# A graph network's first layer: the edge loop in steps of two groups, with eight gathers in a row

## The chip, the cores and the metric

The kernel runs on one core of a Trainium2 chip. The metric is the device time of one execution in microseconds, the median of several runs. A core has five engines with their own instruction streams: PE (matrix products), DVE (vector), ACT (scalar), POOL (GpSimd) and SP (here it only starts transfers). They meet at semaphores: an instruction adds one (`then_inc`) when it is done, and another engine's instruction waits until a count is reached (`wait_ge`). An indirect DMA, the gather of 128 rows by a list of indices, is issued by POOL, which generates its descriptors.

## The reference

Two graph layers, each followed by a residual sum and a layer norm, over 6250 nodes with 128 values and 100000 edges sorted by their destination. Only the first is touched by the change:

```python
h = x @ W1 + b1
h_i, h_j = h[dst], h[src]
e = concatenate([h_i, h_j - h_i], axis=-1)
m = relu(relu(e @ W2 + b2) @ W3 + b3)
out = relu(segment_max(m, dst, num_segments=N_NODES))
x = layernorm(x + out)
# second layer: segment_sum(edge_weight * x[src]) over dst, times W, plus b
```

## The kernel before

The first product is split: for an edge, `e @ W2` is a sum of p (from the destination) and q (from the source). Both tables are computed once and stored, as `p_tab` and `q_tab`. The 100000 edges are 784 tiles of 128, and four tiles are a group: 196 groups of 512 edges (`G`). The first layer's loop works through them, software-pipelined across the engines. For each group:

- POOL gathers q of the sources, four gathers of 128 rows (L423), into one of 12 ring places (`qg`, `RING`).
- SP loads four windows of p of 128 rows each (64 KB, L494, for the group four ahead), and a row of destinations and segment starts spread over the partitions (128 KB, L479).
- DVE makes a one-hot matrix from that row (`oh`, L888). PE adds the two parts in PSUM (`m_ps`): eight passes of the gathered q through the identity and of the window through the one-hot matrix (L1372, L1373). Its last matmul adds one to `m1_done`.
- ACT applies the relu (L635); PE multiplies by W3 (`z_ps`, L1385); ACT applies the second relu (L640); DVE runs the segmented maximum along the edges (the scan, L989); PE transposes (`t_ps`, L1394); ACT copies (L646) and stores (L650).

Beside it, the same loop prepares the second layer: it sorts edges by the block of their source. DVE makes one-hot matrices of the source block (`blk_oh`, L894). PE counts and ranks with them in `s_ps` (L1346 to L1353). DVE turns the counts into the first row of each block (L900, L905, L910). PE adds these first rows with one more matmul, L1359, `first_b` against three times the identity. DVE picks each edge's place by a product and a sum (L916, L918). Once in four groups five small steps (L941 to L960) split places into rows and columns, in each group L967 makes a one-hot matrix of the rows, and PE moves the edge values to their places (`values`, L1332); DVE sums them up (L973).

Each engine runs its own `step0(i, r)` with its parts at fixed lags, so the order of the instructions is written out by hand. On PE a step is: `gathered` (group r-2), `firsts_added` (r-2), `values` (r-7), `slots` (r-1), `second` (r-3), `by_edge` (r-4). Six of PE's parts end in a release for each group. DVE's `one_hot` waits for `m1_done` of two groups before; POOL waits for `m1_done` of twelve groups before:

```python
for g in range(G):
    if g >= RING:
        pool.wait_ge(m1_done, g - RING + 1)
    for j in range(GT):
        ... indirect_dma_start(...)
```

POOL starts the first 48 gathers once q is stored and the first transposes are copied (`tr_copied`). At that time the preparation is still running: DVE counts and places the destinations (L834 to L860), PE sums over partitions (L1282 to L1286) and moves p's rows to their nodes (L1295), and ACT copies them (L618, L627; the last step adds to `p_ev`, 13 in all). SP then writes `p_tab`, and the loop's windows are read from it.

## Time and profile before

| what | value |
|---|---|
| median of 3 runs | 2623.38 us (2616.09 to 2624.47) |
| profiled execution, its own time | 2633.35 us |
| its span, first to last instruction | 2631.6 us |
| mean granted clock of TensorE | 0.917 of full speed |
| busy: PE, DVE, ACT, POOL | 1940.8, 1619.5, 817.0, 1279.1 us |
| chain that ended last, by engine | PE 43%, issue 19%, SP's queue 11%, another core or unknown queue 9%, DVE 8% |
| gathers L423 | 784, mean 971 ns, idle before them 503.2 us |
| relu L635 | 196, mean 687 ns, idle before them 644.2 us |

A "busy" time adds what an engine ran; the chain follows the last instruction back through what released it. "Remote" is a wait whose end the profile can't tie to an instruction that had just ended; "issue" is idle time in which no wait shows. Of the span, the preparation is roughly the first 215 us, the first layer's loop follows until about 1415 us, and the second layer takes the rest.

### The profile page before, as it was taken

Reading aid. Unit: us, or ns where it says so; the run is one execution under the profiler, and the core shown is the slowest. Engines: PE = TensorE matmul, PEld = TensorE weight load, DVE = VectorE, ACT = ScalarE, POOL = GpSimd, SP = SyncE. Lnnn points to the kernel's source line nnn. Section 1 sums busy time; section 2 is a strip of 40 time slices with the busy share of each in tenths; the row PEclk is TensorE's granted clock in tenths of the full one; section 3 lists DMA queues with packets and bytes.
Section 4 is the critical chain, followed back from the end, with each engine's and each line's share of the span. In section 5 each row is a group of like instructions: output and inputs, shape, how many; then the busy total and the mean of one; then the engine's idle time right before and its main releaser. Section 6 shows DMA issues by size and latency. Waiting matters only on the chain.

```text
span 2631.6 us, 62039 instructions
## 1 busy us (share of the span) xinstructions
PE 1940.8 (74%) x15568; PEld 1701.2 (65%) x15568; DVE 1619.5 (62%) x4450; ACT 817.0 (31%) x2385; POOL 1279.1 (49%) x1300
## 2 busy tenths in 40 slices
PE   4616677777777777777785378888888888788884
PEld 4615565565565555565564378877888778788884
DVE  3416666666666666666679544444444444688887
ACT  0312233233332332332332234445554555100003
POOL 6444566666666666666643435555555555100000
PEclk7757999999999999999997589999999999899997
DMA  4215555555555555555553156766666677788885
GB/s 114 81 46 153 142 148 147 151 148 148 150 147 150 146 150 151 146 148 150 148 147 91 32 179 209 216 207 208 216 214 210 214 214 217 225 268 267 262 266 175
DMA packets 534341, 447.34 MB, mean 170 GB/s; under 512 B 64731, under 2 KB 499383, under 8 KB 534240
## 3 DMA queue, kind: packets, MB, share of 16 engines
q1 hardware_dynamic: 342788, 208.10, 29.1%
q0 software_dynamic: 53312, 138.17, 16.5%
q10 hardware_dynamic: 138140, 100.06, 12.7%
q14 instruction: 78, 0.64, 0.1%
q8 instruction: 23, 0.38, 0.1%
HBM read 300.43 MB, written 145.64 MB: 170 GB/s over the span
## 4 chain that ended last, share of the span: by engine, by line
PE 43%; issue 19%; SPq 11%; another core or an unknown queue 9%; DVE 8%; ACT 3%; DMA 2%; DVEq 2%; POOL 2%; ACTq 1%; POOLq 0%
SPq L494 8%; PE z_ps L1385 5%; PE t_ps L1394 4%; PE m_ps L1372 4%; PE z_ps L1460 4%; PE t_ps L1460 4%; PE m_ps L1484 4%; PE m_ps L1373 4%; PE z_ps L1484 3%; PE t_ps L1484 2%; DVE run L989 2%; POOL whole L430 2%; SPq L490 1%; SPq L483 1%
## 5 line engine op out<-in xcount | busy, mean ns | idle before, releaser
L423 POOL DMA_INDIRECT whole<-q_tab,src_ti x784 | 760.9, 971 | 503.2 <-remote 243.0
L440 POOL DMA_INDIRECT tab<-whole,row_at x392 | 410.1, 1046 | 355.9 <-ACT whole L698 175.3
L1119 DVE TENSOR_SCALAR whole<-row_bc,node_id 128x768 f32<-128x768 uint8 x392 | 233.5, 638 | 390.1 <-PE t_ps L1460 110.4
L1460 PE MATMUL z_ps<-win,whole 128*128 128x128 f32 x2352 | 302.9, 286 | 71.6 <-DVE whole L1119 21.8
L1372 PE MATMUL m_ps<-ident,whole 128*128 128x128 f32 x1568 | 324.3, 290 | 29.1 <-issue 17.1
L635 ACT ACTIVATE m<-m_ps,bias 128x512 f32<-128x512 f32 x196 | 134.7, 687 | 644.2 <-remote 591.9
L1460 PEld LDWEIGHTS z_ps<-win,whole 128*128 128x128 f32 x2352 | 282.7, 198 | 78.0 <-issue 41.6
L1460 PE MATMUL t_ps<-win,whole 128*128 128x128 f32 x2352 | 294.7, 280 | 50.6 <-issue 25.8
L1373 PE MATMUL m_ps<-oh,win 128*128 128x128 f32 x1568 | 316.2, 285 | 0.6 <-issue 0.6
L1460 PEld LDWEIGHTS t_ps<-win,whole 128*128 128x128 f32 x2352 | 274.4, 193 | 54.1 <-issue 30.3
L1372 PEld LDWEIGHTS m_ps<-ident,whole 128*128 128x128 f32 x1568 | 259.1, 207 | 62.6 <-issue 62.5
L1170 DVE TENSOR_TENSOR whole<-whole 128x384 f32<-128x384 f32 x440 | 242.9, 552 | 55.9 <-issue 39.3
L916 DVE TENSOR_TENSOR scratch<-s_ps,blk_oh 128x196 f32<-128x196 f32 x196 | 70.6, 360 | 308.1 <-remote 287.3
L1373 PEld LDWEIGHTS m_ps<-oh,win 128*128 128x128 f32 x1568 | 252.3, 202 | 1.3 <-issue 1.3
L989 DVE TENSOR_TENSOR_SCAN run<-row_bc,run,z_ps 128x512 f32<-128x512 uint8 x195 | 248.4, 1274 | 0.7 <-ACT z_ps L640 0.7
L698 ACT ACTIVATE whole<-z_ps,slot_vals 128x128 f32<-128x128 f32 x588 | 169.5, 378 | 221.5 <-PE t_ps L1460 89.2
L1385 PE MATMUL z_ps<-m,w 128*128 128x512 f32 x392 | 232.6, 677 | 0.0
L1394 PEld LDWEIGHTS t_ps<-ident,run 128*128 128x128 f32 x784 | 111.3, 153 | 187.0 <-issue 169.9
L698 ACT ACTIVATE whole<-t_ps,slot_vals 128x128 f32<-128x128 f32 x588 | 168.5, 388 | 137.4 <-PE t_ps L1460 52.3
L1394 PE MATMUL t_ps<-ident,run 128*128 128x128 f32 x784 | 157.3, 297 | 72.7 <-issue 65.0
L1332 PE MATMUL s_ps<-whole 128*128 128x18 bf16 x784 | 48.5, 171 | 198.1 <-issue 163.7
L1332 PEld LDWEIGHTS s_ps<-whole 128*128 128x128 bf16 x784 | 36.8, 96 | 226.4 <-issue 225.5
(277 smaller groups left out, 3128.3 us busy)
## 6 DMA issues: line engine op xcount, KB each, us to landing
win<-p_tab SPq DMA_DIRECT2D x784, 64.0 KB
seg_tab<-run_e ACTq DMA_DIRECT2D x196, 256.0 KB
win<-xw_tab SPq DMA_DIRECT2D x784, 64.0 KB
whole<-tab SPq DMA_DIRECT2D x220, 200.0 KB
whole<-tab ACTq DMA_DIRECT2D x220, 200.0 KB
row_bc<-seg_row_tab SPq DMA_DIRECT2D x196, 128.0 KB
row_bc<-rel_tab SPq DMA_DIRECT2D x196, 96.0 KB
whole<-q_tab,src_ti POOLq DMA_INDIRECT x784
```

What stands on the lines that cost most here:

```text
L423: pool.indirect_dma_start(qg[:, g % RING, j, :], None, q_tab[:, :], IOA(ap=src_ti[:, t:t + 1], axis=0)).then_inc(q_ld[g % RING], 16)
L440: pool.indirect_dma_start(tab[:, :], IOA(ap=row_at[0:FR, k:k + 1], axis=0), fat[0:FR, k % RR, :], None).then_inc(fat_st[k % RR], 16)
L698: last = nc.scalar.activation(fat[0:FR, GK * (r % UN) + c, q * KW:q * KW + D], fat_bank[r % 2][0:FR, c, q * P:(q + 1) * P], ACT.Copy, scal ...
L989: V.tensor_tensor_scan(run[:, s, :], row_bc[:, r % RB, GE:2 * GE], z_ps[:, s, :], first, ALU.mult, ALU.max).then_inc(run_done, 1)
L1119: last = V.tensor_scalar(pick[:, s, j, :], row_bc[:, r, 0:GK * SLOTS], node_id[:, j:j + 1], None, ALU.is_equal)
L1170: V.tensor_tensor(node_hot[:, r % PS, :, :], node_row[:, ds(at, P)].unsqueeze(1).to_broadcast([P, SL, P]), loaded[:, r % PL, 0:SL * KW].re ...
L1372: mm(m1_ps[:, s, c], lhsT=qg[:, r % RING, j, :], rhs=ident[:], start=True, stop=False)
L1373: last = mm(m1_ps[:, s, c], lhsT=win[:, r % UN, j, :], rhs=oh[:, s, c], start=False, stop=True)
L1385: mm(z_ps[:, s, :], lhsT=w3[:], rhs=m1[:, s, :], start=True, stop=True).then_inc(z_done, 1)
L1394: last = nc.tensor.transpose(t_ps[:, s, c], run[:, s, c], ident[:])
L1460: last = mm(fat_bank[s][0:FR, c, q * P:(q + 1) * P], lhsT=pick[:, s, j, (c * SL + q) * FR:(c * SL + q + 1) * FR], rhs=win[:, r % UN, CK * ...
L1484: last = mm(sum_bank[r % PS], lhsT=node_hot[:, r % PS, q, :], rhs=loaded[:, r % PL, q * KW:q * KW + D], start=q == 0, stop=q == SL - 1)
```

## The change

The loop goes in steps of two groups, a pair. The parts and their arithmetic stay, but these move:

- POOL gathers eight times in a row, and asks for one release a pair: `m1_done` of four pairs before. (A line near the top sets `AHEAD` to 3 and a later line sets it to 4; the loop is built with 4.) It begins when all of `p_ev` has arrived, at the end of p's placement.
- Destination rows are loaded for two groups at once (256 KB) into a ring of six pairs, one-hot matrices are made for two groups at once, the slot work of DVE (counts, first rows, product, sum, small steps, the one-hot matrix of rows) is done for two groups at once, and the small steps come once for a pair.
- The first rows are added on DVE, two additions that read PSUM, and the matmul L1359 with its release is gone.
- On PE a step is `gathered` a and b, `second` of the pair before, `by_edge` and `values` of two before, and `slots` of this pair. `slots` and `values` release once for a pair. DVE's step begins with a wait for the `slots` of the pair before.
- SP writes `p_tab` before it loads the destination rows.

```diff
@@ POOL
-            pool.wait_ge(tr_copied, 1)
...
-            for g in range(G):
-                if g >= RING:
-                    pool.wait_ge(m1_done, g - RING + 1)
-                for j in range(GT):
+            pool.wait_ge(p_ev, HX // GT)
...
+            for u in range(G // 2):
+                if u >= AHEAD:
+                    pool.wait_ge(m1_done, 2 * (u - AHEAD) + 2)
+                for g in (2 * u, 2 * u + 1):
+                    for j in range(GT):
...
@@ SP
-            for g in range(G + LATE):
-                if g + UN < G:
-                    sp.wait_ge(m1_done, g + 1)
-                    windows(p_tab, g + UN)
...
+            for v in range(G // 2 + 2):
+                if 2 * v + UN < G:
+                    sp.wait_ge(m1_done, 2 * v + 2)
+                    for g in (2 * v + UN, 2 * v + UN + 1):
+                        windows(p_tab, g)
+                if v >= 2 and 2 * (v - 2) + RB < G:
+                    sp.wait_ge(run_done, 2 * (v - 2) + 2)
+                    rows0(v - 2 + RB // 2)
@@ ACT
+            def step0(i, w):
+                for h in range(2):
+                    for part, lag in ((relu_1, 1), (relu_2, 2)):
+                        if runs(i, 2 * (w - lag)):
+                            part(i, 2 * (w - lag) + h)
+                if runs(i, 2 * (w - 1)):
+                    many_copy(i, w - 1)
+                for h in range(2):
+                    if runs(i, 2 * (w - 3)):
+                        run_copy(i, 2 * (w - 3) + h)
+                        store(i, 2 * (w - 3) + h)
@@ DVE, first rows and places of a pair
+            def slots_of(i, w):
...
+                V.tensor_tensor_scan(first[...], keep[...], rows3[...], 0.0, ALU.mult, ALU.add).then_inc(slot_step, 1)
+                for s in range(2):
+                    last = V.tensor_tensor(picked[...], s_ps[:, s, 0:GT * NBK]..., first[...], ALU.add)
...
+                V.tensor_tensor(picked[:, :, :], picked[:, :, :], blk_oh[:, a:a + 2, :, :]..., ALU.mult).then_inc(slot_step, 1)
+                V.tensor_reduce(slot_t[...], picked[:, :, :], axis=AX_X, op=ALU.add).then_inc(slot_done, 1)
@@ DVE
+            def step0(i, w):
+                if runs(i, 2 * (w - 1), RING):
+                    dve.wait_ge(slot_ps, pair(i, w - 1) + 1)
+                if runs(i, 2 * (w - 3), RING):
+                    values_sum(i, w - 3)
+                if runs(i, 2 * (w - 1), RING):
+                    slots_of(i, w - 1)
+                if runs(i, 2 * (w - 2), RING):
+                    for h in range(2):
+                        scan(i, 2 * (w - 2) + h)
+                if runs(i, 2 * (w + 1), RING):
+                    one_hot(i, w + 1)
+                    block_hot(i, w + 1)
+                if runs(i, 2 * (w - 1), RING):
+                    slots_placed(i, w - 1)
@@ PE
-            def firsts_added(i, r):
...
-                for part, lag in ((gathered, 2), (firsts_added, 2), (values, PERM_LAG + 1), (slots, 1), (second, 3), (by_edge, 4)):
-                    if runs(i, r - lag, RING):
-                        part(i, r - lag)
+                for part, lag in ((gathered, 0), (second, 1), (by_edge, 2)):
+                    if runs(i, 2 * (w - lag), RING):
+                        for h in range(2):
+                            part(i, 2 * (w - lag) + h)
+                if runs(i, 2 * (w - 2), RING):
+                    values(i, w - 2)
+                if runs(i, 2 * w, RING):
+                    slots(i, w)
```

POOL's stream from its last preparation gathers on, before; L412 is the preparation's gather, L423 the loop's:

```order
L412 DMA slot_vals<-dst_tab,tile_i 128x128 x6
L423 DMA whole<-q_tab,src_ti 128x128 [waits tr_copied,q_st]
L423 DMA whole<-q_tab,src_ti 128x128 x47
L423 DMA whole<-q_tab,src_ti 128x128 [waits m1_done]
L423 DMA whole<-q_tab,src_ti 128x128 x3
```

POOL's stream at the same place after; L419 is the loop's gather:

```order
L408 DMA slot_vals<-dst_tab,tile_i 128x128 x6
L419 DMA whole<-q_tab,src_ti 128x128 [waits p_ev,q_st]
L419 DMA whole<-q_tab,src_ti 128x128 x31
L419 DMA whole<-q_tab,src_ti 128x128 [waits m1_done]
L419 DMA whole<-q_tab,src_ti 128x128 x7
```

The first run goes from 48 gathers to 32 and waits for `p_ev`; each later run goes from four to eight.

PE's stream for one group in the middle of the loop, before, from the end of `gathered` to the end of the step (`m_ps` first product, `s_ps` slots and values, `z_ps` second product, `t_ps` transposes):

```order
L1373 MATMUL m_ps<-oh,win 128x128
L1359 MATMUL s_ps<-first_b,three_b 128x196
L1332 MATMUL s_ps<-whole 128x18 x4
L1346 MATMUL s_ps<-blk_oh,ones_b 128x98
L1347 MATMUL s_ps<-blk_oh,ones_b 128x98
L1348 MATMUL s_ps<-unit_b,ones_b 128x98
L1351 MATMUL s_ps<-ones_b,blk_oh 49x1 x4
L1352 MATMUL s_ps<-blk_oh,after_b 128x196
L1353 MATMUL s_ps<-blk_oh,ones_b 128x2x49
L1385 MATMUL z_ps<-m,w 128x512
L1394 MATMUL t_ps<-ident,run 128x128 x4
```

PE's stream for one pair at the corresponding place, after:

```order
L1350 MATMUL m_ps<-whole,win 128x128
L1362 MATMUL z_ps<-m,w 128x512 x2
L1371 MATMUL t_ps<-ident,run 128x128 x8
L1313 MATMUL s_ps<-whole 128x18 x8
L1328 MATMUL s_ps<-blk_oh,ones_b 128x98
L1329 MATMUL s_ps<-blk_oh,ones_b 128x98
L1330 MATMUL s_ps<-unit_b,ones_b 128x98
L1333 MATMUL s_ps<-ones_b,blk_oh 49x1 x4
L1334 MATMUL s_ps<-blk_oh,after_b 128x196
L1335 MATMUL s_ps<-blk_oh,ones_b 128x2x49
```

`firsts_added` is gone, `second` and `by_edge` come as pairs ahead of `values` and `slots`, and the six slot rows come twice (the second time they are followed by the next `gathered`).

DVE's stream for one group, before, at the loop's last groups (`third`, `rows`, `first_b`: first rows; `scratch`, `late`: product and sum; `run`: the scan):

```order
L888 TENSOR_SCALAR oh<-row_bc,iota_p 128x512
L989 SCALAR_TENSOR_TENSOR run<-row_bc,run,z_ps 128x512
L916 TENSOR_TENSOR scratch<-s_ps,blk_oh 128x196
L918 TENSOR_REDUCE late<-scratch 128x4
L900 TENSOR_SCALAR third<-s_ps 128x98
L905 TENSOR_SCALAR rows<-third 128x2x49
L910 SCALAR_TENSOR_TENSOR first_b<-keep,rows 128x100
L894 TENSOR_TENSOR blk_oh<-iota_f,blk_t 128x196
L967 TENSOR_TENSOR whole<-iota_f,whole 128x512
```

DVE's stream for one pair, after, up to the small steps:

```order
L965 TENSOR_REDUCE slot_vals<-s_ps 128x24
L907 TENSOR_SCALAR third<-s_ps 128x196
L909 TENSOR_SCALAR rows<-third 128x4x49
L912 SCALAR_TENSOR_TENSOR first<-keep,rows 128x200
L916 TENSOR_TENSOR scratch<-s_ps,first 128x196 x2
L921 TENSOR_TENSOR scratch<-scratch,blk_oh 128x392
L923 TENSOR_REDUCE late<-scratch 128x8
L977 SCALAR_TENSOR_TENSOR run<-whole,run,z_ps 128x512 x2
L895 TENSOR_SCALAR whole<-whole,iota_p 128x1024
L901 TENSOR_TENSOR blk_oh<-iota_f,blk_t 128x392
L946 TENSOR_SCALAR whole<-late 128x8
```

The scans stood ahead of the slot work and now stand behind it, the two additions (L916) are new, and the one-hot matrices of the next pair follow the scans.

## Rows read from the trace of the kernel before

**Rows 1.** The page's busy us, share of the span and instructions of each engine

```profile
PE 1940.8 (74%) x15568; PEld 1701.2 (65%) x15568; DVE 1619.5 (62%) x4450; ACT 817.0 (31%) x2385; POOL 1279.1 (49%) x1300
```

**Rows 2.** One line's instructions: ns min/median/max, first and last start us

```profile
L635 ACT ACTIVATE m<-m_ps,bias x196: 687/687/690, 218.7 to 1408.9; 128x512 f32<-128x512 f32 x196
...
L423 POOL DMA_INDIRECT whole<-q_tab,src_ti x784: 938/945/1919, 113.2 to 1359.9; - x196
```

**Rows 3.** Busy us (x) of PE, PEld, DVE, ACT, POOL; clock, DMA share, GB/s

```profile
400.00:600.00 200.00, 149.02 (x1164) 114.66 (x1165) 138.16 (x348) 60.88 (x128) 125.62 (x130) 0.95 0.55 148
1370.00:1400.00 30.00, 29.48 (x264) 24.33 (x263) 28.18 (x76) 13.46 (x29) 0.00 (x0) 0.98 0.51 143
```

**Rows 4.** Groups of instructions, 400 to 1300 us: busy us, mean ns | idle

```profile
L423 POOL DMA_INDIRECT whole<-q_tab,src_ti x582 | 564.0, 969 | 335.7 <-remote 198.3 <-issue 133.2 <-PE m_ps L1373 4.2
...
L635 ACT ACTIVATE m<-m_ps,bias 128x512 f32<-128x512 f32 x145 | 99.6, 687 | 499.5 <-remote 489.7 <-PE m_ps L1373 9.7
...
L989 DVE TENSOR_TENSOR_SCAN run<-row_bc,run,z_ps 128x512 f32<-128x512 uint8 x146 | 186.0, 1274 | 0.0
...
L910 DVE TENSOR_TENSOR_SCAN first_b<-keep,rows 128x100 bf16<-128x100 f32 x145 | 53.2, 367 | 5.0
L916 DVE TENSOR_TENSOR scratch<-s_ps,blk_oh 128x196 f32<-128x196 f32 x145 | 52.5, 362 | 240.2 <-remote 234.0 <-PE s_ps L1359 6.2
...
L900 DVE TENSOR_SCALAR third<-s_ps 128x98 f32<-128x98 f32 x145 | 36.3, 250 | 0.0
...
L960 DVE TENSOR_TENSOR whole<-whole 128x288 bf16<-128x288 f32 x37 | 17.0, 458 | 6.0 <-issue 6.0
```

**Rows 5.** Timeline of one group: start us, us, instruction [idle before <-releaser]

```profile
695.50 0.39 PE L1373 MATMUL m_ps<-oh,win 128*128 128x128 f32 x2
...
698.19 0.24 PE L1332 MATMUL s_ps<-whole 128*128 128x18 bf16 x4 [2.21 <-issue]
...
697.95 0.94 POOL L423 DMA_INDIRECT whole<-q_tab,src_ti  x1 [0.30 <-issue]
700.31 0.94 POOL L423 DMA_INDIRECT whole<-q_tab,src_ti  x1 [1.43 <-remote]
...
700.08 0.69 ACT L635 ACTIVATE m<-m_ps,bias 128x512 f32<-128x512 f32 x1 [3.89 <-remote]
```

**Rows 6.** Timeline around a run of eight gathers, POOL, ACT and DVE

```profile
245.31 0.95 POOL L423 DMA_INDIRECT whole<-q_tab,src_ti  x1 [1.88 <-remote]
...
247.81 1.32 POOL L423 DMA_INDIRECT whole<-q_tab,src_ti  x1 [0.30 <-issue]
...
257.31 0.94 POOL L423 DMA_INDIRECT whole<-q_tab,src_ti  x1 [1.77 <-remote]
...
247.05 0.69 ACT L635 ACTIVATE m<-m_ps,bias 128x512 f32<-128x512 f32 x1 [0.67 <-issue]
...
257.15 0.69 ACT L635 ACTIVATE m<-m_ps,bias 128x512 f32<-128x512 f32 x1 [1.03 <-remote]
...
247.64 0.68 DVE L967 TENSOR_TENSOR whole<-iota_f,whole 128x512 bf16<-128x512 f32 x1
```

**Rows 7.** Waits, 110 to 205 us: us in total, times, longest us

```profile
DVE run_e L834 <- issue: 10.1, 11, 2.1
```

**Rows 8.** Timeline of the preparation, DVE, PE, POOL and ACT

```profile
142.99 0.18 DVE L845 SCALAR_TENSOR_TENSOR start<-tile_of,below 128x14 f32<-128x14 f32 x1 [8.34 <-remote]
...
181.02 0.18 DVE L847 TENSOR_TENSOR full<-s_ps,start 128x21 f32<-128x21 f32 x1 [37.86 <-remote]
...
145.62 0.59 PE L1283 MATMUL s_ps<-start,corner 128*128 128x21 f32 x2
...
171.95 0.94 POOL L423 DMA_INDIRECT whole<-q_tab,src_ti  x1 [0.30 <-issue]
...
203.57 0.66 ACT L627 ACTIVATE whole<-m_ps 128x512 f32<-128x512 f32 x1
```

**Rows 9.** Busy us behind an idle time of PE, columns as in rows 3

```profile
698.00:702.00 4.00, 3.81 (x21) 2.56 (x22) 3.30 (x10) 1.35 (x3) 2.27 (x3) 0.59 0.54 143
```

More of the change, by code:

```diff
@@ L340, in i_of, with pair @@
             return n // UN * i + r // UN
+        def pair(i, w, n=RING):
+            return n // 2 * i + w
         def runs(i, r, n=UN):
@@ L1355, in firsts_added @@
[L1355 to L1359 removed]
+                if old(i, 2 * (w - 1), RING):
+                    pe.wait_ge(vals_in, pair(i, w - 1) + 1)
+                pe.wait_ge(perm_ready, pair(i, w) + 1)
```

347 lines of the change are left out of this document (149 added, 198 removed).

## The prediction, made before the changed kernel was run

> **What bounds the kernel now.** I began with the busy shares of the page [rows 1]. No engine fills the span: PE is busy 74%, DVE 62%, POOL 49%. So I looked for the stage that the change touches. The relu that follows each group's first matmuls, L635, runs 196 times from 218.7 to 1408.9 us [rows 2], and POOL's gathers, L423, run 784 times, four for each group, from 113.2 to 1359.9 us [rows 2]. The first layer's loop is thus about 1190 us of the span. Two stretches of it differ [rows 3]. While POOL gathers (400 to 600 us), PE is busy 149.0 of 200 us and DVE 138.2. After the last gather (1370 to 1400 us) PE is busy 29.5 of 30 us. In time per group: between 400 and 1300 us there are 582 gathers, so 145.5 groups in 900 us, 6.19 us each [rows 4]; from the last gather's start to the last relu there are 12 groups (the ring is 12 deep) in 49.0 us, 4.1 us each, and 48.1 us from that gather's end, 4.0 us each [rows 2]. PE can do a group in 4.0 us; with gathers beside it a group takes 6.19 us.
>
> What sets 6.19? Four gathers at 0.969 us are 3.88, three pauses of 0.30 between them 0.90, and the wait ahead of the first is (198.3 + 4.2)/145 = 1.40 us [rows 4, 5]: 6.18 us. So the loop runs at the pace of POOL plus one wait for `m1_done`. Yet the matmuls that POOL waits for are over by then. In the timeline a group's last m_ps matmul ends at 695.50 + 0.39 = 695.89 us; ACT's relu that needs it starts at 700.08, POOL's next gather at 700.31, and POOL's fourth gather ended at 697.95 + 0.94 = 698.89 us [rows 5]. Everybody who waits for PE's releases gets them together, 1.2 us behind the run of gathers. ACT loses 489.7 us to such "remote" waits in 900 us, and DVE at L916 234.0 [rows 4]. I read it so: while POOL generates the gathers' descriptors, PE's releases arrive late, mostly after the run. A longer run has a longer tail: the run of eight from 245.31 is followed by an idle time of 1.77 us [rows 6], and the run of 48 that ends at 171.95 + 0.94 = 172.89 is followed by DVE's L847 only at 181.02, which had waited 37.86 us for a matmul begun at 145.62 and lasting 0.59 [rows 8], so 8.1 us of tail.
>
> Of that late release the Trainium skill's page "Perfetto Trace Analysis", section "Per-instruction lifecycle: what the profiler-reported window actually captures", says that TensorE's window closes at an estimated end and hides the semaphore's travel. By that rule part of the 4.2 us could be matmuls that end later than shown; the sum, which uses only starts on POOL, ACT and DVE, would be the same but the gain from fewer releases would be less sure.
>
> **The change, part by part.** I take as the end of the stage the last relu, 1408.9 us, and build it anew from POOL's side. Later stages keep their work.
>
> (1) *The gathers leave the preparation.* POOL now waits for the end of p's placement before it gathers. Before, 48 gathers ran in it. What they held up, from the rows: DVE's L834 steps have 11 idle times of 10.1 us in all [rows 7]; L845 waits 8.34, L847 37.86 [rows 8]. Together 56 us at most. Some hops and PE's own work stay, so 50 us is my value, and 30 us the lower bound: the 34.8 us from the end of L1283's matmul (145.62 + 0.59) to L847, less 5 for something that is late next. Behind it come the copies of the placement on ACT, whose last starts at 203.57 [rows 8] and ends at 204.2. So POOL starts at 204.2 - 50 = 154 us and not at 113.2.
>
> (2) *The head start is given up.* The first 32 gathers need no release (four pairs ahead): 32 x (0.969 + 0.30) = 40.6 us, to 195 us, and then a tail between that of the run of eight (1.5 us, 1.77 less the 0.26 of the start) and that of 48 (8.1): 5.5 us by the straight line between them. So the 94 remaining pairs begin at about 200 us. Before, POOL's waiting groups began at 1360.8 - 184 x 6.19 = 222 us.
>
> (3) *The period of a pair, P.* Eight gathers 8 x 0.969 = 7.75, seven pauses 2.1, and one wait. With the wait of a run of four, 1.40, P is 11.26 us; with that of the run of eight, 1.77, it is 11.6. The one run of eight that the trace shows whole went from 245.31 to 257.31, 12.00 us [rows 6], since two of its gathers were stretched. I take 12.0 plus the stretch of (4), 12.1 us. Now: 12.37 us for two groups. The saving of one wait, 1.40, is mostly eaten by the longer tail and by stretched gathers. 94 x 12.1 = 1137 us. The lower end is DVE's work. It is busy 138.2 us per 32.3 groups, 8.55 us per pair [rows 3]. The first rows added on DVE are two additions of the form of L916, 0.36 each; its five small steps (L941 to L960, the longest 0.46) come each pair instead of each two pairs, which at half that length each is 0.6 to 0.7 more [rows 4]. So 10.0 us. Were releases never late, P would be near that. Upper end: 13.0 to 14.0, under the rivals.
>
> (4) *Wider DVE instructions beside gathers.* The gather at 247.81 took 1.32 us instead of 0.94 while DVE's L967 (from 247.64, 0.68 us) ran beside its start [rows 6]. L967's form becomes twice as wide, 1.37 us. Mean against shortest gather is 0.969 against 0.938 [rows 2, 4], so all stretching is worth 0.25 us per pair now; one blocker twice as long is met no oftener but may cost up to double: 0.1 is taken, 0 to 0.25 the bounds, 0 to 24 us in all. The Trainium skill's page "SBUF — State Buffer", section "SBUF: two separate sides", says that a DVE instruction in a two-port mode and a GpSimd one hold their shared port pair exclusively, the loser blocked for the whole instruction. The trace agrees in this one gather; by the rule at its worst each wide instruction would hold one gather its full length, 1.4 us per pair or 129 us, by the rows' mean 9.
>
> (5) *The tail of the stage.* The last four pairs need no more gathers: 8 x 4.0 = 32 us, where 12 groups took 48.
>
> (6) *On PE.* The L1359 matmul (0.25 us each) and the release behind it go: 8 releases for two groups instead of 12. PE had 51 us free in 200 [rows 3], so its work is hidden. Windows and rows change from per-group to per-pair transfers of the same bytes; with DMA at a share of 0.55 [rows 3] I cost them at nothing, covered by windows being asked for four groups early; without that cover a wait on `win_ld` shows on PE.
>
> Sum: 154 + 40.6 + 5.5 + 1137 + 32 = 1369 us for the last relu instead of 1408.9: 39 us less. The profiled execution took 2633.35 us (span 2631.6), so it would take 2594; it stands 10 us above the median of the runs, 2623.4, and from that I predict 2584 us.
>
> **Rivals.** *A: releases come more freely.* With fewer of them in flight, the wait stays 1.40 and nothing is stretched: P = 11.3, 75 us less, 2509 us. With DVE's 10.0 as the bound, 197 us less, 2387. For it: groups with POOL idle take 4.0. Against it: the tail grew with the run each time that the trace shows it.
>
> *B: slower, the release of `slot_ps` heads a chain that no longer fits.* DVE's new step begins with a wait for the slots of the pair before, the last of PE's eight releases. Behind it are queued on DVE: values_sum 0.2, the slot steps at double width (2 x 0.25 for L900 and as much for L905 behind it, 2 x 0.37 for L910, 0.72 for the additions, 0.72 and 0.71 for the product and the sum behind them) 3.9, two scans 2.55 [rows 4]: 6.6 us. PE's second matmul of the pair waits for those scans, then two L1385 pairs, the transposes and slots follow, and the next gathered: by the end phase's 8.0 us of PE per pair less what can stand ahead, 2.8 + 3.6. That makes 13.0 us if that release comes at the end of each run of gathers. PE then also stands idle for some 5 us a pair: after an idle time of 2.21 us up to 698.19 [rows 5] the granted clock of the next 4 us was 0.59, the 1.2 GHz level for most of it [rows 9]; 4 x 0.41 = 1.6 us of PE's full speed went. Were 1 us of that on the chain, P = 14.0. For it: in the 12.00 us of that run of eight only one group's relu passed, at 247.05, and the next was ACT's at 257.15 [rows 6]; two must pass now. Against it: releases did trickle through in that run. The time: P = 13.0 gives +85, 2669; 14.0 gives +179, 2763. It decides from P = 12.1 + 39/94 = 12.5 us on.
>
> *C: the preparation gives back little.* If only 15 of the 50 us come, because the waits there have another cause, and P is 12.1, the sum is -4 us: 2619. For it: those waits are "remote", their cause inferred. Against it: they end right after the gathers do.
>
> **How the numbers follow.** Forecast (P 11.7 to 12.4, 2547 to 2612) 0.42; A 0.16; B 0.34; C 0.08. A change under 0.3% (8 us) can't be told from none here. Faster is A and nearly all of the forecast, 0.56; the same is C and the forecast's edge, 0.09; slower is B and a little of C, 0.35. Range with one in five left out: 2495 (A without its DVE-bound part) to 2715 (B to P = 13.5).
>
> **What would show it.** In the changed profile: no gather before about 150 us, and DVE's L847 successor waiting microseconds, not 38; the first relu near 160; runs of eight gathers and one idle time of 1.8 to 2.3 us ahead of each; 8 gathers per 12.1 us between 400 and 1300 us; last relu near 1370. Rival B shows as a POOL that waits 3 us or more per pair and a PE with a lower granted clock and long waits for DVE's scans; A as pairs of 11.3 us or less. I am wrong if the idle time between runs is far from 2 us, or if the first gather is later than 175 us.

## The result: 5% slower

The changed kernel takes 2755.2 us (median of 4 runs, 2746.8 to 2770.1), the kernel before 2623.9 beside it; the ratio is 1.050, with a 95% interval of 1.045 to 1.055. The forecast was 2584 us, with a range of 2495 to 2715. Its profiled execution took 2770.1 us, with a span of 2768.1, 136.5 us more than the span before.

First the page: the busy shares and the chain of waits.

```profile
PE 2021.0 (73%) x15372; PEld 1733.6 (63%) x15372; DVE 1641.1 (59%) x4107; ACT 816.9 (30%) x2287; POOL 1338.6 (48%) x1298
...
PE 28%; DVE 22%; issue 18%; another core or an unknown queue 15%; SPq 11%; DVEq 3%; DMA 2%; ACT 1%; ACTq 0%; POOL 0%; POOLq 0%
```

Against [rows 1], DVE is busy 22 us longer, POOL 60 and PE 80. Where the stage lies is told by the relu of the m_ps products (L633 now) and the loop's gathers (L419 now); columns as in [rows 2].

```profile
L633 ACT ACTIVATE m<-m_ps,bias x196: 687/687/691, 160.5 to 1530.7; 128x512 f32<-128x512 f32 x196
...
L419 POOL DMA_INDIRECT whole<-q_tab,src_ti x784: 938/944/3789, 142.8 to 1491.3; - x196
```

The first relu is 58.2 us earlier than in [rows 2], the last one 121.8 us later. The rest of the kernel, behind the last relu, took 1237.4 instead of 1222.7 us, 14.7 us more. So the loop itself, from its first relu to its last, took 1370.2 us instead of 1190.2, 180 us more, and the preparation gave 58 of them back. By stretch, columns as in [rows 3]:

```profile
400.00:600.00 200.00, 142.24 (x990) 105.33 (x989) 125.74 (x258) 53.88 (x101) 118.89 (x115) 0.85 0.47 130
1500.00:1540.00 40.00, 31.17 (x249) 23.12 (x248) 34.08 (x73) 15.12 (x29) 0.00 (x0) 0.93 0.27 79
```

While POOL gathers, DVE is busy 126 of 200 us, 12 less than in [rows 3], and the granted clock is 0.85 instead of 0.95. With the gathers over, from 1500 us on, PE is busy 31.2 of 40 us, where it was busy 29.5 of 30 in [rows 3]. The groups of instructions between 400 and 1300 us, columns as in [rows 4]:

```profile
L419 POOL DMA_INDIRECT whole<-q_tab,src_ti x520 | 547.5, 1053 | 353.5 <-PE m_ps L1350 211.2 <-issue 138.8 <-remote 3.5
...
L1362 PE MATMUL z_ps<-m,w 128*128 128x512 f32 x260 | 206.0, 919 | 183.1 <-DVE run L977 104.6 <-issue 78.1
...
L953 DVE TENSOR_TENSOR whole<-iota_f,whole 128x1024 bf16<-128x1024 f32 x65 | 79.3, 1220 | 0.0
...
L965 DVE TENSOR_REDUCE slot_vals<-s_ps 128x72 f32 x65 | 15.1, 233 | 291.1 <-remote 255.7 <-PE s_ps L1335 35.0 <-issue 0.2
```

520 gathers are 65 pairs, so a pair takes 900/65 = 13.85 us. It is eight gathers of 1.053 us, 8.42, seven pauses of 0.305, 2.13, and one wait of (211.2 + 3.5)/65 = 3.30 us: 13.85. The waits of the same stretch (us in total, times, longest):

```profile
DVE slot_vals L965 <- remote: 255.7, 52, 12.7
...
POOL whole L419 <- PE m_ps L1350: 211.2, 63, 6.6
...
PE z_ps L1362 <- DVE run L977: 104.6, 52, 4.4
PE z_ps L1362 <- issue: 78.1, 35, 4.4
```

In [rows 4] POOL's wait ended "remote", behind matmuls that had been over for a while. Now it ends with L1350 itself: PE does the products that POOL waits for only after the run of gathers. The timeline of one pair shows it (start us, us, instruction, idle time before):

```profile
706.35 0.39 PE L1350 MATMUL m_ps<-whole,win 128*128 128x128 f32 x2
709.84 1.10 PE L1362 MATMUL z_ps<-m,w 128*128 128x512 f32 x2 [3.10 <-DVE run L977]
...
715.90 0.21 PE L1335 MATMUL s_ps<-blk_oh,ones_b 128*128 128x98 bf16 x1
...
716.67 0.65 PE L1350 MATMUL m_ps<-whole,win 128*128 128x128 f32 x2
718.40 0.27 PE L1349 MATMUL m_ps<-ident,whole 128*128 128x128 f32 x1 [1.08 <-issue]
719.10 0.27 PE L1349 MATMUL m_ps<-ident,whole 128*128 128x128 f32 x1 [0.43 <-issue]
...
722.05 0.39 PE L1350 MATMUL m_ps<-whole,win 128*128 128x128 f32 x2
...
708.34 0.94 POOL L419 DMA_INDIRECT whole<-q_tab,src_ti  x1 [1.06 <-PE m_ps L1350]
...
717.47 0.94 POOL L419 DMA_INDIRECT whole<-q_tab,src_ti  x1 [0.30 <-issue]
722.71 0.94 POOL L419 DMA_INDIRECT whole<-q_tab,src_ti  x1 [4.30 <-PE m_ps L1350]
...
705.07 0.23 DVE L965 TENSOR_REDUCE slot_vals<-s_ps 128x72 f32 x1 [1.99 <-remote]
...
720.16 0.23 DVE L965 TENSOR_REDUCE slot_vals<-s_ps 128x72 f32 x1 [5.75 <-remote]
...
713.34 0.69 ACT L633 ACTIVATE m<-m_ps,bias 128x512 f32<-128x512 f32 x1 [0.56 <-PE z_ps L1362]
```

POOL's run goes from 708.34 to 718.41 us. PE comes as far as 717.3 in it, to half of the next group's m_ps products, and then stands. Single matmuls follow at 718.40 and 719.10, and from 720.04 on it runs at full pace. The last product begins at 722.05, and POOL's next run at 722.71. DVE gets the slots' release at 720.16; the last matmul that it stands for was over at 715.90 + 0.21 = 716.11. It waits 5.75 us there, 4.05 of them behind that matmul's end. Its waits of the stretch that end "remote" come to 3.9 us a pair (255.7/65). Not every release is late: ACT's relu at 713.34, in the middle of the run, follows a z_ps product that had just ended. And between 400 and 1300 us PE is busy 652.8 us; of its 247 us of idle time, 183.1 stand ahead of the z_ps products of L1362, 104.6 of them as a wait for DVE's scans.

In the preparation:

```profile
119.24 0.18 DVE L854 TENSOR_TENSOR full<-s_ps,start 128x21 f32<-128x21 f32 x1 [0.78 <-PE s_ps L1264]
...
141.41 0.67 ACT L625 ACTIVATE whole<-m_ps 128x512 f32<-128x512 f32 x1
...
156.72 0.77 PE L1349 MATMUL m_ps<-ident,whole 128*128 128x128 f32 x2 [15.64 <-DMA whole<-q_tab,src_ti]
...
190.11 0.95 POOL L419 DMA_INDIRECT whole<-q_tab,src_ti  x1 [0.30 <-issue]
```

The successor of L847 waits 0.78 us instead of 37.86 [rows 8], p's placement ends at 142.1 instead of 204.2, and the first product starts at 156.72 us. The fifth run of gathers, the first that needs a release, begins at 190.11 us, behind an idle time of 0.30 us like that between any two gathers.

### The profile page after: what moved, and what is told of

It is laid out like the page before. It is cut to its first block, busy times and chain, and to the rows that moved or that the text cites. A ratio compares the mean times of both kernels' runs of the same rounds, so it can differ in the third digit from the quotient of the medians.

```text
span 2768.1 us, 60133 instructions
## 1 busy us (share of the span) xinstructions
PE 2021.0 (73%) x15372; PEld 1733.6 (63%) x15372; DVE 1641.1 (59%) x4107; ACT 816.9 (30%) x2287; POOL 1338.6 (48%) x1298
## 4 chain that ended last, share of the span: by engine, by line
PE 28%; DVE 22%; issue 18%; another core or an unknown queue 15%; SPq 11%; DVEq 3%; DMA 2%; ACT 1%; ACTq 0%; POOL 0%; POOLq 0%
SPq L491 8%; DVE run L977 5%; PE m_ps L1466 4%; PE z_ps L1442 4%; PE z_ps L1362 4%; PE z_ps L1466 3%; PE t_ps L1442 3%; PE t_ps L1466 2%; DVE whole L895 2%; DVE first L912 2%; DVE scratch L921 2%; PE t_ps L1371 1%; SPq L480 1%; DVE scratch L916 1%
## 5 line engine op out<-in xcount | busy, mean ns | idle before, releaser
L419 POOL DMA_INDIRECT whole<-q_tab,src_ti x784 | 825.5, 1053 | 575.1 <-PE m_ps L1350 309.5
L1362 PE MATMUL z_ps<-m,w 128*128 128x512 f32 x392 | 308.7, 912 | 270.9 <-DVE run L977 157.2
L1350 PE MATMUL m_ps<-whole,win 128*128 128x128 f32 x1568 | 338.2, 291 | 73.4 <-issue 71.7
L1362 PEld LDWEIGHTS z_ps<-m,w 128*128 128x128 f32 x392 | 85.8, 256 | 383.8 <-issue 363.1
L1350 PEld LDWEIGHTS m_ps<-whole,win 128*128 128x128 f32 x1568 | 259.3, 204 | 74.6 <-issue 73.3
L965 DVE TENSOR_REDUCE slot_vals<-s_ps 128x72 f32 (+1 forms) x98 | 22.8, 233 | 427.4 <-remote 376.5
L977 DVE TENSOR_TENSOR_SCAN run<-whole,run,z_ps 128x512 f32<-128x512 uint8 x195 | 248.8, 1276 | 13.0
L653 ACT ACTIVATE whole<-s_ps 49x4 f32 (+1 forms) x98 | 16.4, 167 | 800.9 <-DVE late L923 736.3
L1371 PEld LDWEIGHTS t_ps<-ident,run 128*128 128x128 f32 x784 | 125.5, 180 | 93.3 <-issue 90.7
L633 ACT ACTIVATE m<-m_ps,bias 128x512 f32<-128x512 f32 x196 | 134.7, 687 | 160.8 <-issue 112.4
L1466 PE MATMUL m_ps<-whole 128*128 128x128 f32 x1056 | 135.3, 278 | 11.1 <-DVE whole L1151 11.1
```

The source lines that it names most:

```text
L419: pool.indirect_dma_start(qg[:, g % RING, j, :], None, q_tab[:, :], IOA(ap=src_ti[:, t:t + 1], axis=0)).then_inc(q_ld[g % RING], 16)
L977: V.tensor_tensor_scan(run[:, s, :], edge_row[:, r % RB, GE:2 * GE], z_ps[:, s, :], first, ALU.mult, ALU.max).then_inc(run_done, 1)
L1350: last = mm(m1_ps[:, s, c], lhsT=win[:, r % UN, j, :], rhs=edge_oh[:, r % UN, c], start=False, stop=True)
L1362: mm(z_ps[:, s, :], lhsT=w3[:], rhs=m1[:, s, :], start=True, stop=True).then_inc(z_done, 1)
L1466: last = mm(sum_bank[r % PS], lhsT=node_hot[:, r % PS, q, :], rhs=loaded[:, r % PL, q * KW:q * KW + D], start=q == 0, stop=q == SL - 1)
```

## The experiments

The kernel before did not take 2624 us in every session. In sessions 1 to 3, 5 and 7 (experiments 1 to 9, 13, 14, 16, 17) it took 2207 to 2210 us, in the others 2598 to 2630. In the first kind no wait of the loop ends "remote" between 400 and 1000 us, and POOL's waits for PE are at most 1.5 us in these 600 (25.4 in experiment 3), so I call it "releases on time"; the second kind, in which the result above was measured, "releases late". Ratios are to the kernel before of the same session. Experiments 4, 13 and 17 are one kernel, as are 1 and 14: the repeats were meant for a session with late releases and did not get one.

**1 and 14, scans first** (on time both times).

```diff
@@ DVE step0
+                if runs(i, 2 * (w - 2), RING):
+                    for h in range(2): scan(i, 2 * (w - 2) + h)
                 if runs(i, 2 * (w - 1), RING):
                     dve.wait_ge(slot_ps, pair(i, w - 1) + 1)
...
-                if runs(i, 2 * (w - 2), RING):
-                    for h in range(2): scan(i, 2 * (w - 2) + h)
```

> The changed kernel with one edit on DVE: the two scans come ahead of the wait for the slots' release and of the slot work, not behind them. Chain theory (the pair's period is the chain slots' release, DVE's slot work 3.3 us, two scans, PE's second products, transposes, slots, late release): the second products no longer stand behind the slot work, the period falls from 13.85 us to about 12.3 and, with 94 such periods, the time by 130 to 170 us, to about 2600. Run-length theory (eight gathers in a row let only five or six of PE's releases through, the order of the rest doesn't matter): period stays within 0.3 us of 13.85, time 2730 to 2760.

> The changed kernel with the scans ahead of DVE's wait for the slots' release, as in the first experiment, which fell on a chip with releases on time (2247 against 2276 for the changed kernel unedited). Meant for a chip with late releases. Chain theory: period 12.3 instead of 13.85 us, about 2600. Run-length theory, which the relayed pair of runs now favours: the period stays at 13.3 to 13.9, 2700 to 2760.

2246.8 and 2247.2 us, ratios 1.0165 (1.013 to 1.020) and 1.018 (1.015 to 1.021). Against the 1.029 of the changed kernel (experiment 5) it gains 29 us, which says nothing yet on late releases. POOL doesn't wait here either, but its gathers are shorter, 1.006 us in experiment 1 and 0.983 in 14, against 1.038 in experiment 5:

```profile
L419 POOL DMA_INDIRECT whole<-q_tab,src_ti x466 | 458.1, 983 | 142.0 <-issue 142.0
```

**2, slots early, and 3, both orders** (on time).

```diff
@@ PE step0
-  gathered(w), second(w-1), by_edge(w-2), values(w-2), slots(w)
+  gathered(w), values(w-2), slots(w), second(w-1), by_edge(w-2)
```

> The changed kernel with one edit on PE: values and slots come right behind gathered, ahead of second and by_edge. Chain theory: the slots' release leaves PE some 3 us earlier in the step, but the second products still stand behind the slot work and the scans on DVE; the period falls by 0.5 to 1.5 us, time 2620 to 2710. Run-length theory: no change, 2730 to 2760.

> Both edits of order together (DVE: scans first; PE: values and slots behind gathered). Chain theory: neither chain is longer than the run of gathers any more, the period is that of POOL, eight gathers and one wait: 11.6 to 12.0 us, time 2550 to 2590, faster than the kernel before. Run-length theory: 2730 to 2760.

2273.5 us, 1.030 (1.028 to 1.033), and 2298.4 us, 1.040 (1.037 to 1.043). Slots early gives nothing, and with the scans first it costs 52 us against the scans alone. My expectation missed there: PE's next values then wait for DVE's slot work of the same step (L1313 for L923, 110.9 us between 400 and 1000 us in experiment 3).

**4, 13 and 17, the kernel before with eight gathers in a row** (on time all three times).

```diff
             for g in range(G):
-                if g >= RING:
-                    pool.wait_ge(m1_done, g - RING + 1)
+                if g >= RING and g % 2 == 0:
+                    pool.wait_ge(m1_done, g - RING + 2)
```

> The kernel before with one edit on POOL: it waits for m1_done once for two groups, so eight gathers stand in a row, ten groups ahead at the least; the group-wise order of PE, DVE and ACT stays. Chain theory: the group-wise step has no such long chain, two groups take 12.0 to 12.4 us, time 2590 to 2630. Run-length theory: in a run of eight PE gets through little more than one group's six releases, so two groups take 13.5 us or more, time 2720 or more.

> The kernel before with eight gathers in a row, as in the fourth experiment, which fell on a chip with releases on time (2207 against 2209 us). Meant for a chip with late releases (the kernel before at 2600 or more). Run-length theory: a run of eight holds PE back for 11.7 us and two groups need twelve releases, so two groups take 13.5 us or more instead of 12.37, time +110 us or more. Chain theory: the group-wise order doesn't mind, 12.0 to 12.4 us, -35 to 0 us. On a chip with releases on time: no change again.

> The kernel before with eight gathers in a row, once more in the hope of a chip with late releases (the kernel before at 2600 us or more). Run-length theory: two groups take 13.0 us or more instead of 12.37, because a run of eight keeps PE's releases back for 11.7 us and PE gets through one group's step and a little more, time +60 us or more. Rival (only the pair-wise order suffers): 12.0 to 12.4 us, -35 to 0 us. Where releases are on time: no change, 2208.

Ratios 0.999 (0.998 to 1.001), 1.001 (0.999 to 1.002) and 0.998 (0.996 to 0.999). With releases on time POOL waits for nothing, so its runs have no ends. What eight in a row cost the old order with releases late was not measured, so no run separates the length of the runs from the pair-wise order there.

**5, the changed kernel again** (on time, no edit).

> The changed kernel itself, unedited, beside the kernel before on one chip, because the kernel before took 2209 us on the chip of the first four experiments, not 2624. If the late releases of PE are what the change loses by, then on a chip where the kernel before takes 2209 us (releases on time) POOL gathers without a wait in both kernels and the changed one is within 2% of the one before, 2190 to 2260 us; on a chip where the one before takes 2620, it is 5% slower again, 2740 to 2770. If the order of its work makes it slow by itself, it is 5% slower on either.

2275.6 us, 1.029 (1.025 to 1.033): slower in this kind of session too, by 66 us. The loop's gathers, first in the kernel of experiment 4, which here stands for the kernel before (it takes the same time), then in the changed one; columns as in [rows 2]:

```profile
L423 POOL DMA_INDIRECT whole<-q_tab,src_ti x784: 940/944/2510, 81.2 to 1103.6; - x196
```

```profile
L419 POOL DMA_INDIRECT whole<-q_tab,src_ti x784: 940/947/3794, 108.9 to 1167.2; - x196
```

The changed kernel starts its gathers 27.7 us later and ends them 63.6 us later. The other 36 us are in the gathers themselves. The same two in that order between 400 and 1000 us:

```profile
L423 POOL DMA_INDIRECT whole<-q_tab,src_ti x464 | 459.0, 989 | 141.4 <-issue 141.1 <-PE m_ps L1373 0.3
```

```profile
L419 POOL DMA_INDIRECT whole<-q_tab,src_ti x448 | 464.9, 1038 | 136.6 <-issue 136.0 <-PE m_ps L1350 0.6
```

Both wait for nothing but the pauses, and a gather takes 1.038 instead of 0.989 us; over 784 gathers that is 38 us. 28 + 38 = 66, against 63.6 at the last gather.

**6 and 7, no gathers after the first twelve groups** (on time; one run each). Both leave part of the computation out: PE uses the rows of the first twelve groups again and again.

```diff
@@ POOL, changed kernel
-            for u in range(G // 2):
-                if u >= AHEAD:
+            for u in range(RING // 2):
+                if u >= RING:
@@ POOL, kernel before
-            for g in range(G):
+            for g in range(RING):
@@ PE, both
-                pe.wait_ge(q_ld[r % RING], 16 * GT * (i + r // RING + 1))
+                pe.wait_ge(q_ld[r % RING], 16 * GT)
```

> The changed kernel with the gathers after the first twelve groups left out (those groups' rows are used again, so this part of the computation is left out). It shows the pair's period without POOL. Chain theory: the pair step alone takes 9.3 us as in the last pairs of the changed kernel, so about 94 x (13.85 - 9.3) = 430 us less than the changed kernel on a chip with late releases, and 94 x 1 = 100 us less on the other. Run-length theory: the same, since no gather holds a release.

> The kernel before with the gathers after the first twelve groups left out in the same way (this part of the computation is left out). Expected from its last twelve groups: 3.9 to 4.0 us per group, 8.0 us for two, so the group-wise step without POOL is 1.3 us per pair shorter than the pair-wise one, 120 us in all. If the pair-wise step were the shorter one by itself, this would come out longer than the changed kernel without gathers.

2174.5 and 2072.5 us. The relus, changed kernel first:

```profile
L633 ACT ACTIVATE m<-m_ps,bias x196: 687/687/692, 129.1 to 1070.4; 128x512 f32<-128x512 f32 x196
```

```profile
L635 ACT ACTIVATE m<-m_ps,bias x196: 687/687/690, 125.8 to 978.4; 128x512 f32<-128x512 f32 x196
```

195 steps of one group in 941.3 and 852.6 us: 9.65 against 8.74 us for two groups. With no gathers behind the first twelve groups the pair-wise order is 0.9 us slower for two groups, some 90 of the 102 us. I expected 1.3.

**8, the kernel before with gathers after the placement** (on time).

```diff
-            pool.wait_ge(tr_copied, 1)
+            pool.wait_ge(p_ev, HX // GT)
```

> The kernel before with one edit: POOL waits for the end of p's placement before its first gather, as the changed kernel does. On a chip with late releases (the kernel before at 2620 us): my step (1) says the preparation ends some 60 us earlier (first gather near 143, first relu near 160 instead of 218.7), but 48 gathers (61 us) now come behind it, so the loop's last relu moves by -10 to -20 us, time 2600 to 2615. On a chip with releases on time (the kernel before at 2209 us), where the gathers hold up nothing, it only starts POOL 28 us later: 2235 us, +1.2%. Rival (the gathers of the preparation hold up nothing on either chip, the waits there have another cause): +25 to +30 us on both.

2233.6 us, 1.012 (1.010 to 1.015): with releases on time the early gathers held up nothing, and the later start costs 26 us. Its gathers:

```profile
L423 POOL DMA_INDIRECT whole<-q_tab,src_ti x784: 940/944/2640, 108.0 to 1124.9; - x196
```

**9, the changed kernel with early gathers** (on time): the same two lines the other way round.

> The changed kernel with its start of the gathers undone: they begin when the first transposes are copied, as in the kernel before. On a chip with late releases: the first 32 gathers hold the preparation up again until about 155 us plus a tail, so first relu near 200 and time 2760 to 2800, against 2755. On a chip with releases on time: the gathers start 28 us earlier and the time falls from 2276 to 2248, which leaves the other 40 us over the kernel before to the order of the pair's work. Rival (start of the gathers doesn't matter): 2276.

2259.4 us, 1.021 (1.018 to 1.025), 16 us better than experiment 5 and not 28: the gathers start at 81.6 us, 27 us earlier, but their mean between 400 and 1000 us is 1.052 us instead of 1.038.

**10 to 12, one release made late on purpose** (late). After each run of gathers POOL waits for `slot_ps` and passes it on:

```diff
@@ POOL, behind each run of gathers
+                if u >= AHEAD:
+                    pool.wait_ge(slot_ps, u - AHEAD + 1)
+                    pool.sem_inc(slot_rel, 1)
@@ DVE
-                    dve.wait_ge(slot_ps, pair(i, w - 1) + 1)
+                    dve.wait_ge(slot_rel, pair(i, w - 1) + 1)
```

> The changed kernel with one release made late on purpose: DVE doesn't wait for PE's slot_ps but for a second semaphore that POOL adds to once a run of eight gathers is done and slot_ps has come. It imitates, for this one release, what the trace of the first chip shows for all. Chain theory (this release heads the chain through DVE's slot work, scans and PE's second products): where releases are otherwise on time, the pair's period rises from 10.66 us to 12.5 to 14, time 2450 to 2590. Run-length theory: one release in eight hardly matters, period at most 11.2, time under 2330.

> The same with the scans ahead of DVE's wait (the edit of the first experiment), which takes the second products out of the chain behind the late release. Chain theory: the period falls again by 1.5 us or more against the changed kernel with the relayed release, to 10.7 to 12 us, time 2280 to 2400. Run-length theory: no difference between the two.

> The kernel before with the same release made late: POOL passes slot_ps on to DVE's L900 after each run of four gathers. Chain theory: the group-wise step has more slack behind this release, since its scans stand ahead of the wait and only first rows hang on it: two groups take 10.4 to 11.2 us, time 2210 to 2290, so the same lateness costs the group-wise order less than half of what it costs the pair-wise one. Rival (lateness costs both orders alike): two groups take 12.5 us or more.

The three ran where releases come late (the kernel before: 2598.3 us). The changed kernel itself was not run beside them. 10 took 2706.8 us, 1.043 (1.037 to 1.049), 11 took 2700.0, 1.040 (1.028 to 1.052), 12 took 2933.2, 1.130 (1.125 to 1.135). The waits of 10, then of 11 with two of its groups of instructions:

```profile
DVE slot_vals L972 <- POOLq L423: 267.2, 63, 12.0
...
POOL whole L420 <- PE m_ps L1357: 188.2, 62, 6.2
...
PE z_ps L1369 <- DVE run L984: 123.0, 66, 4.3
```

```profile
POOL whole L420 <- PE m_ps L1357: 189.0, 47, 6.5
...
PE m_ps L1357 <- issue: 62.3, 106, 1.9
PE m_ps L1356 <- issue: 62.0, 107, 1.3
...
L1369 PE MATMUL z_ps<-m,w 128*128 128x512 f32 x268 | 159.5, 722 | 2.9 <-issue 2.7
L1378 PE MATMUL t_ps<-ident,run 128*128 128x128 f32 x531 | 83.8, 285 | 76.5 <-ACT run_e L651 44.3 <-issue 32.1
```

With the scans first, PE's z_ps products no longer wait for a scan: the idle time ahead of them was 196.5 us in experiment 10 (123.0 for the scans, 73.3 "issue") and is 2.9 us now. The pair's period stayed: 535 and 531 gathers in 900 us, 13.5 and 13.6 us each. Most of that idle time went elsewhere on PE: ahead of the m_ps products it rose from 47.3 to 127.8 us, nearly all "issue", and ahead of the transposes from 0 to 76.5, 44.3 of it a wait for ACT's copy. In all, PE's idle time fell from 243.6 to 206.4 us, and its products took the 37 us instead: PE is busy 693.6 us at a granted clock of 0.84, against 656.4 at 0.87. POOL's wait for PE did not move, 188 and 189 us. So taking DVE's scans out of PE's way did not shorten the pair where releases are late. That PE would stand in a run of gathers whatever stands ahead of it is my reading of the idle time that moved. That the relay costs nothing in 10 fits, since the release was late anyway. In 12 it costs 13%:

```profile
DVE third L907 <- POOLq L427: 390.8, 115, 5.7
...
POOL whole L424 <- PE m_ps L1380: 335.8, 115, 5.7
```

POOL waits 335.8 us for PE's products and DVE 390.8 for POOL. The group-wise order suffers more from this late `slot_ps` than the pair-wise one. My expectation for it was wrong.

**15, the changed kernel, POOL asks for each group** (late).

```diff
             for u in range(G // 2):
-                if u >= AHEAD:
-                    pool.wait_ge(m1_done, 2 * (u - AHEAD) + 2)
                 for g in (2 * u, 2 * u + 1):
+                    if u >= AHEAD:
+                        pool.wait_ge(m1_done, g - 2 * AHEAD + 1)
```

> The changed kernel with one edit undone on POOL: it waits for m1_done of one group (eight groups before) ahead of every four gathers, not for two groups ahead of eight; all else stays pair-wise. Run-length theory (eight gathers in a row hold PE back): where releases are late, the two releases of a pair's m_ps come in different gaps, POOL's runs are four long as before, and the pair takes 12.4 to 13.0 us instead of 13.85, 80 to 130 us less than the changed kernel, some 2630 to 2680. Order theory (the pair-wise order of PE and DVE loses the time whatever the runs): 13.5 us or more, 2700 to 2760. Where releases are on time, POOL waits for nothing and this runs like the changed kernel, 2276 us.

2673.8 us, 1.016 (1.009 to 1.023). Of the 5.0% that the change loses, 3.4 are back by this edit (two runs, and each ratio is to the kernel before of its own session). But the runs did not get shorter. Its gathers between 400 and 1300 us, and three of them:

```profile
L419 POOL DMA_INDIRECT whole<-q_tab,src_ti x556 | 584.7, 1052 | 316.7 <-PE m_ps L1350 167.2 <-issue 148.2 <-remote 1.3
```

```profile
703.74 0.94 POOL L419 DMA_INDIRECT whole<-q_tab,src_ti  x1 [2.10 <-PE m_ps L1350]
...
712.79 0.95 POOL L419 DMA_INDIRECT whole<-q_tab,src_ti  x1 [0.30 <-issue]
716.83 0.95 POOL L419 DMA_INDIRECT whole<-q_tab,src_ti  x1 [3.09 <-PE m_ps L1350]
```

From 703.74 to 713.7 us eight follow each other: the second group's release is there before the fourth gather ends. POOL merely begins at the first group's release and not at the second's, and waits (167.2 + 1.3)/69.5 = 2.42 us per pair instead of 3.30. With the same 1.052 us per gather that is 12.95 us per pair instead of 13.85, and 94 x 0.9 = 85 us. The time was as the run-length theory had it, the way was not.

**16, the widest DVE instruction cut into four** (on time).

```diff
-                V.tensor_tensor(row_hot[:, s, :, :], ...)
+                for k in range(0, ST, 2):
+                    V.tensor_tensor(row_hot[:, s, k:k + 2, :], ...)
```

> The changed kernel with its widest DVE instruction, the one-hot matrix of rows (L953, 1024 wide, 1.22 us), cut into four of 256. Port theory (gathers that meet it are stretched: their mean is 1.04 to 1.06 us against 0.97 to 0.99 in the kernel before): the mean gather falls by 0.04 us or more, and with 784 of them the time by 30 us or more where POOL is never waiting (2276 to about 2240), by 20 to 40 us where it is (about 2755 to 2725). Rival (the stretch comes from the gathers' own addresses or the DMA's load): mean gather unchanged, time unchanged or some us longer for the three extra instructions.

2245.7 us, 1.015 (1.012 to 1.019), 30 us less than experiment 5, with

```profile
L419 POOL DMA_INDIRECT whole<-q_tab,src_ti x468 | 458.5, 980 | 142.6 <-issue 141.4 <-PE m_ps L1351 1.2
```

0.980 us per gather instead of 1.038, less than the 0.989 of the kernel before. This doesn't make the one wide instruction the whole stretch: experiment 14 leaves it as wide, moves it by the scans, and has 0.983. What counts is whether a gather begins while it runs, as in this pair of the changed kernel (late):

```profile
712.63 1.22 DVE L953 TENSOR_TENSOR whole<-iota_f,whole 128x1024 bf16<-128x1024 f32 x1
...
713.43 1.24 POOL L419 DMA_INDIRECT whole<-q_tab,src_ti  x1 [0.31 <-issue]
```

The gather begins 0.42 us before L953 ends and takes 0.30 us more than 0.94. In experiment 5, between 400 and 1000 us, 46 of the 448 gathers begin while L953 runs, with 0.78 us of it left on average, and take 0.65 us more; they hold 30.0 of the 43.7 us above 0.94. In experiment 14 such gathers number 57, but only 0.40 us is left of it, and they take 0.28 us more. The 112 gathers of experiment 5 that begin while a scan (L977) runs take 0.03 us more. The section "SBUF: two separate sides" of the Trainium skill's page "SBUF — State Buffer" says that a DVE instruction with two SBUF inputs, as L953 has, and a GpSimd one that reads SBUF can't hold their shared port pair together, and that the later one is blocked until the first is done. The traces agree for gathers that begin while L953 runs: 0.65 us more with 0.78 us left of it.

**18, the kernel before with narrow one-hot matrices** (late): L888 and L967 in two halves each.

> The kernel before with its two widest one-hot instructions (L888 and L967, 512 wide) cut into two of 256 each, as a version that might beat both kernels. Port theory: where releases are on time POOL never waits and every nanosecond of a gather counts 784 times; the mean gather falls from 0.99 to 0.96 or less, time from 2209 to 2175 to 2195. Where releases are late: the same 0.02 to 0.03 us per gather, at most 20 us less. Rival (two more instructions per group on DVE lengthen the releases' chains): same or up to 1% slower.

2635.9 us, 1.002 (1.000 to 1.004). Its gathers took 0.962 instead of 0.969 us:

```profile
L423 POOL DMA_INDIRECT whole<-q_tab,src_ti x582 | 559.7, 962 | 340.2 <-remote 197.9 <-issue 133.2 <-PE m_ps L1377 9.1
```

No gain. No version here beats the kernel before by more than 0.2% in the kind of session in which it was measured.

## Why the prediction was wrong

Its steps, in its order:

- *What bounds the kernel before*: POOL and one wait, 6.18 us per group. It holds for the session of the profile; the late release is real, and it has no fixed place in the kernel, since in other sessions the same program runs without it, 415 us faster.
- *(1) The gathers leave the preparation*: right in kind, and larger than its own upper bound. The placement ends 62 us earlier, where "56 us at most" was given and 50 taken, so POOL starts at 142.8 us (154 forecast); the wait of 37.86 us is gone. What this step alone is worth where releases are late, no run shows. Experiment 8 has it alone where they are on time: there it costs 26 us.
- *(2) The head start*: the size was right by luck. From POOL's start to the fifth run took 47.3 us, forecast 40.6 + 5.5 = 46.1. The tail of 5.5 us did not appear (0.30 us of idle time ahead of the 33rd gather); instead the first four gathers took 10.9 us, not 3.9. The run begins at 190 us and not at 200 because of (1).
- *(3) The period of a pair*: this is the step that failed. Forecast 12.1 us, measured 13.85, over 94 pairs 165 us too little. Rows of one run of eight gave the wait ahead of the next as 1.77 us, a release that came late. It is 3.30. That late release was not what POOL waited for: 211.2 of the 214.7 us end with the product itself. I had taken it that PE would always have done the products for which POOL waits by the end of the run. In that run of eight PE had to do one group; now it must do two, does not get through, and POOL waits for matmuls that are done after the run, two groups of them, because it asks for the second. Asking for the first alone gives 0.9 us of the 1.5 back (experiment 15).
- *(4) Wide instructions beside gathers*: too small. Over the shortest gather, 0.938 us, the 12.1 held 0.73 us of stretch a pair (0.25 in the old mean, 0.38 more in that run of eight, 0.1 for the change); 8 x (1.053 - 0.938) = 0.92 was measured. It makes up 0.2 of the 1.75 us, the wait 1.53. "Met no oftener" was wrong: between 400 and 1300 us L967 of the kernel before had 37 gathers begin within it in 145 groups, at 0.1 us in all, while L953 has 61 in 65 pairs, at 41.2 us. The stretch before lay at L888 and L910, 7.7 and 7.5 of 16.2 us.
- *(5) The tail of the stage*: 38 us for the last four pairs instead of 32. The 32 were priced at the old order's pace; experiments 6 and 7 give the pair-wise order 0.9 us more a pair, 3.6 of the 6 us. Why it is slower by itself, no run shows.
- *(6) On PE*: its work was to be hidden. It is not: POOL waits for it. And it takes longer, at a granted clock of 0.85 (400 to 600 us); L1362 takes 0.92 us each, L1385 before took 0.68. That was in rival B.
- Not in the sum: 14.7 us behind the loop.

Sum with the measured terms: 1408.9 + 94 x 1.75 - 39 + 6 - 10 = 1530 us for the last relu; 1530.7 was measured. (The -10 is the earlier start.)

Rival B had the time (P = 14.0, 2763 us), one true reason, that two groups must pass where the trace showed one, and all three of its signs: POOL waits over 3 us a pair, the granted clock is lower, and PE waits long for DVE's scans (104.6 us in 900). But that chain, from the slots' release through DVE's scans, is not enough for the period: in experiment 11, against 10, the scans are taken out of it and the period stays, as far as a relayed release can stand for a natural one. What remains open: why PE stands inside a long run, whether its releases under way are limited, and what makes releases late in one session and not in another. Experiments 15 and 16 ran on a chip of the same number, one late and one on time, so it is not the chip by its number. The old order with eight in a row and late releases was not measured, nor was the scans' edit without the relay. POOL's distance of four pairs, where the ring has places for six, was not varied either.

## What to carry to other kernels

A wait that is read from one instance in the old kernel (a run of eight with one group's work beside it) is no price for the new one: ask whether the work that has to pass in that time still fits. When one engine waits once for two units, it waits for the second of them; let it wait for each unit at its own place, which here, in one session with late releases, was worth two thirds of the loss. And measure a change whose profile is full of waits without a visible releaser in more than one session: with the gathers behind it the placement ended 62 us earlier in one kind, and in the other the same wait cost 26 us of the kernel's time.

## What the runs showed of the hardware that I had not expected

- The same program takes 2208 us in some sessions and 2624 in others, with little spread inside each. In the late kind, many of PE's releases reach other engines only behind a run of gathers (1.2 us behind it in [rows 5], 4.05 us behind the matmul's end at 720.16 us above); others pass within it (713.34 us). Two groups of the loop take 12.4 instead of 10.3 us, and p's placement ends at 204 us instead of 110 (experiment 4).
- In such a session PE's matmuls themselves stand in a run of gathers and just behind it, with no wait that the profile shows (62 us ahead of the products of one line in 900 us, experiment 11).
- A gather that begins while a 1024 wide DVE instruction runs is held until shortly before that one's end (0.65 us more with 0.78 us left, experiment 5); one that begins within a scan is not (0.03 us). Cutting the wide one into four took 0.058 us off the mean gather (experiment 16 against 5) and 30 us off the time, and moving the scans did as much without narrowing it (0.055 us and 29 us, experiment 14).
